# Attention scores built by adding key differences onto an older bank: one row-maximum product for two key tiles instead of eight

## The reference, cut to what matters

```python
src_trans = (einsum('bsf,of->bso', src, W_src) + b_src) * src_mask[:, :, None]   # keys and values
tgt_trans = (einsum('btf,of->bto', layernorm(x), W_tgt) + b_tgt) * tgt_mask[:, :, None]
scores = einsum('bthd,bshd->bhts', q, k) / sqrt(64)
scores = where(src_mask == 0, -inf, scores)
attn = softmax(scores, axis=-1)
tgt_update = einsum('bhts,bshd->bthd', attn, v)
x = x + tanh(g_xattn) * (concat([tgt, tgt_update]) @ W_out.T + b_out)
x = x + tanh(g_ffn) * bit_linear(silu(conv1d(bit_linear(layernorm(x), w1))), w2)
```

## Time and profile before

| what | value |
|---|---|
| median of 3 runs | 1748.87 us (1747.53 to 1750.27) |
| the profiled execution's own time | 1751.08 us |
| its span | 1749.3 us |
| PE busy | 1644.8 us, 94% |
| DVE, ACT, POOL busy | 1137.5, 836.4, 724.3 us |
| mean granted clock of PE | 0.981 |
| HBM read, written | 124.75 MB, 74.71 MB |

### The profile page before, as it was taken

How to read it: one execution, slowest core, us unless ns; L and a number is a source line. 1 busy time by engine, 2 the same in 40 slices (tenths; PEclk the granted TensorE clock), 3 DMA queues, 4 the chain that set the end, 5 groups by cost and what they waited for, 6 DMA issues and landing times. The chain is left out here.

```text
span 1749.3 us, 23957 instructions
## 1 busy us (share of the span) xinstructions
PE 1644.8 (94%) x8754; PEld 1009.1 (58%) x8754; DVE 1137.5 (65%) x2183; ACT 836.4 (48%) x901; POOL 724.3 (41%) x314
## 2 busy tenths in 40 slices
PE   6999999999998999999999999999999878797978
PEld 5788788888885544455444544454446444454544
DVE  7787634444436667656876677657734977969493
ACT  3233312222210344434564355524565988879776
POOL 1231000000000488856786577756871624426160
PEclk9999999999999999999999999999999989899989
DMA  7787555444434411113132133202143211020302
GB/s 258 267 278 247 195 182 184 164 165 163 161 144 151 152 62 62 65 69 110 62 110 97 57 114 110 86 2 109 54 156 119 71 55 37 23 75 1 97 0 79
DMA packets 109480, 200.88 MB, mean 115 GB/s; under 512 B 9280, under 2 KB 34880, under 8 KB 109376
## 3 DMA queue, kind: packets, MB, share of 16 engines
q1 hardware_dynamic: 109376, 199.50, 32.9%
HBM read 124.75 MB, written 74.71 MB: 114 GB/s over the span
## 5 line engine op out<-in xcount | busy, mean ns | idle before, releaser
L791 POOL TENSOR_TENSOR acc<-acc,pr 128x1024 f32<-128x1024 f32 x188 | 448.7, 2387 | 130.5 <-ACT pr L821 113.9
L821 ACT ACTIVATE pr<-ps,mcol 128x1024 f32<-128x1024 f32 x256 | 284.5, 1115 | 362.9 <-PE ps L1591 357.7
L1110 DVE CUSTOM_DVE_ANT_0 junk<-ps,mbias 128x512 bf16<-128x512 f32 x512 | 333.1, 689 | 129.8 <-PE ps L1566 125.4
L1603 PE MATMUL ps<-pr,vv 128*64 128x512 f32 x1024 | 273.8, 616 | 0.0
L798 POOL TENSOR_TENSOR h_first<-h_first,last_tap 128x1023 f32<-128x1023 f32 x43 | 105.3, 2451 | 177.0 <-DVE h_first L1443 146.4
L772 POOL MEMSET nmt<- 128x128 f32 x1 | 0.2, 205 | 343.4 <-DVE chl L1344 343.4
L1566 PE MATMUL ps<-kh,qh 64*128 64x512 f32 x512 | 123.1, 452 | 11.0 <-DVE nmv L1110 9.8
L791 POOL TENSOR_TENSOR acc<-pr 128x1024 f32<-128x1024 f32 x32 | 76.9, 2402 | 122.5 <-ACT pr L821 122.5
L1566 PEld LDWEIGHTS ps<-kh,qh 64*128 64x128 f32 x512 | 50.9, 184 | 128.7 <-issue 99.4
L1848 PE MATMUL ps<-w2q,hq 128*128 128x512 bf16 x512 | 123.0, 395 | 1.5 <-ACT hq L1002 0.7
L1691 PE MATMUL ps<-xiT,w1q 128*128 128x512 bf16 x512 | 121.2, 380 | 2.7 <-DVE x2t L1472 2.7
(11 more groups left out here) (175 smaller groups left out, 3147.1 us busy)
## 6 DMA issues: line engine op xcount, KB each, us to landing
craw<-in_ctxT SPq DMA_DIRECT2D x8, 2048.0 KB, 8.9
xa<-in_x SPq DMA_DIRECT2D x32, 256.0 KB, 3.9
wraw<-in_w1T SPq DMA_DIRECT2D x16, 512.0 KB, 5.9
wraw<-in_w2T SPq DMA_DIRECT2D x16, 512.0 KB, 6.6
q_split<-kqh SPq DMA_DIRECT2D x32, 256.0 KB, 2.1
q_split<-kql SPq DMA_DIRECT2D x32, 256.0 KB, 2.4
base<-lna SPq DMA_DIRECT2D x32, 256.0 KB, 3.7
k_split<-kqh SPq DMA_DIRECT2D x32, 256.0 KB, 2.0
```

The costliest lines, as they stand in the source:

```text
L791: nc.gpsimd.tensor_tensor(acc[:, blk % 2, :], first, pr[:, (8 * blk + j) % NP, :], ALU.add).then_inc(pool_acc, 1)
L821: act.activation(pr[:, u % NP, :], ps[:, 2 * (u % 2):2 * (u % 2) + 2, :].rearrange("p a t -> p (a t)"), ACT.Exp, bias=mcol[:, (u // 64) * ...
L1110: dve.tensor_tensor_reduce(out=(junk1 if n < LEAD and n % 2 else junk)[:, e, :], in0=ps[:, first_bank(n) + e, :], in1=mbias[:, b % 2, kk * ...
L1603: last = pe.matmul(ps[64 * e:64 * e + 64, 6 + blk % 2, :], vv[g % 2][:, j, 64 * e:64 * e + 64], pr[:, u % NP, e * CH:(e + 1) * CH], start= ...
```

## The change: what it does

For a block of queries, the scores of key tile `j` are now `S_j = S_{j-2} + q·(k_j - k_{j-2})` for `j` from 2 to 7. The banks of unit `u` are those of unit `u-2`, and they still hold `S_{j-2}` with the row maximum in it, so the first matmul doesn't start the bank anew (`start=j < 2 and w == 0`) and the product `aug1·maug` is sent for tiles 0 and 1 alone. Three products are left for the other six.

The differences are made in stage B. For each `m`, once the full key has been rounded (`kqh`, which `pe_tops` still needs), DVE makes the difference to the key tile two before, in two operations of 256 columns (in an odd chunk the first one needs the last 256 columns of the chunk before, kept in `carry`), ACT rounds it (`kdh`) and copies the new `carry`, and DVE makes the remainder. SP stores three parts, and `load_lo` loads three.

For room in SBUF `acc` moves to where `w2q` is loaded later, `vv0` and `kd_hi1` take its place, and `kdh` and `carry` lie over `qh1` and `kh1`. So `load_qk(1)` now stands behind the last chunk's key stores, `load_vv(0)` behind the whole of stage B, and the load of `w2q` also waits for the last `sums`.

```diff
-    kd = nc.dram_tensor("k_split", (B * PAIRS, 2, P, S), F32).ap()
+    kd = nc.dram_tensor("k_split", (B * PAIRS, 3, P, S), F32).ap()
...
             def load_lo(g):
...
+                sp.dma_start(kd_hi[g % 2][:].bitcast(F32), kd[g, 2]).then_inc(sp_lo[g % 2], 16)
...
-                    for w, t in ((0, kqh), (1, kql)):
+                    for w, t in ((0, kqh), (1, kql), (2, kdh)):
...
+                if last and half:
+                    for sl in range(2):
+                        sp.wait_ge(sp_k_out[sl], 48 + 96 * NCH)
+                    sp.wait_ge(act_b, c * B_ACT_N + B_ACT[f"cy{PAIRS - 1}"])
+                    load_qk(1)
...
             load_mrow(0)
-            load_qk(1)
             sp.dma_start(mcol[:], mask_cols).then_inc(sp_mcol, 16)
             load_lo(0)
-            for sl in range(2):
-                sp.wait_ge(sp_v_out[sl], 16 + 32 * (NCH - 1))
-            load_vv(0)
             b_chunk(B - 1, 1, True)
...
             sp.wait_ge(pe_bv, NCH * CT + 8)
+            load_vv(0)
             sp.wait_ge(dve_b, NCH * B_DVE_N)
...
+            sp.wait_ge(pe_z, 2 * NG)
             sp.dma_start(w2q[:], w2q_d.rearrange("(k p) o -> p k o", p=P)).then_inc(sp_w2, 16)
...
                     act.activation(kqh[:, m % 2, :], kq[:, m % 2, :], ACT.Copy).then_inc(act_b, 1)
+                    act.wait_ge(dve_b, c * B_DVE_N + B_DVE[f"db{m}"])
+                    act.activation(kdh[:, m % 2, :], kql[:, m % 2, :].bitcast(F32), ACT.Copy).then_inc(act_b, 1)
+                    act.activation(carry[:, m, :], kq[:, m % 2, 2 * P:CH], ACT.Copy).then_inc(act_b, 1)
...
+            def key_steps(dn, an, m, half):
+                diff, keys = kql[:, m % 2, :].bitcast(F32), kq[:, m % 2, :]
...
+                if half:
+                    dve.tensor_tensor(diff[:, 0:2 * P], keys[:, 0:2 * P], carry[:, m, :], ALU.subtract).then_inc(dve_b, 1)
+                else:
+                    dve.tensor_copy(diff[:, 0:2 * P], keys[:, 0:2 * P]).then_inc(dve_b, 1)
+                dve.tensor_tensor(diff[:, 2 * P:CH], keys[:, 2 * P:CH], keys[:, 0:2 * P], ALU.subtract).then_inc(dve_b, 1)
...
-                terms = ((kh[g % 3][:, keys], qh[g % 3][:, tokens]), (kl[g % 2][:, keys], qh[g % 3][:, tokens]),
-                         (kh[g % 3][:, keys], ql[g % 2][:, tokens]), (aug1[:], maug[g % 2][:, tokens]))
+                terms = ((kd_hi[g % 2][:, keys], qh[g % 3][:, tokens]), (kl[g % 2][:, keys], qh[g % 3][:, tokens]),
+                         (kd_hi[g % 2][:, keys], ql[g % 2][:, tokens]), (aug1[:], maug[g % 2][:, tokens]))
+                if j >= 2:
+                    terms = terms[0:3]
...
-                                         start=w == 0, stop=w == 3)
+                                         start=j < 2 and w == 0, stop=w == len(terms) - 1, skip_group_check=True)
```

More of the change, by code:

```diff
@@ L133, in flamingo_gated_block @@
         maskc = sb("maskc", [P, NCH * CT], F32)
+        kdh = sb("kdh", [P, 2, CH], F32R)
+        carry = sb("carry", [P, PAIRS, 2 * P], F32)
         assert used["at"] <= CRAW
@@ L160, in flamingo_gated_block @@
         used["at"] = TOP_AB
-        vv, ql, kl, maug = [], [], [], []
+        kd_hi, vv, ql, kl, maug = [], [], [], [], []
         for i in range(2):
-            vv.append(sb(f"vv{i}", [P, NT, P], F32))
+            if i == 0:
+                kd_hi.append(sb("kd_hi0", [P, S], F32R))
+            else:
+                vv.append(sb("vv1", [P, NT, P], F32))
             ql.append(sb(f"ql{i}", [P, S], F32R))
@@ L168, in flamingo_gated_block @@
                 assert used["at"] == TOP_AB + SLOT
-                acc = sb("acc", [P, 2, 2 * CH], F32)
+                vv.append(sb("vv0", [P, NT, P], F32))
+                kd_hi.append(sb("kd_hi1", [P, S], F32R))
         mbias = sb("mbias", [P, 2, S], F32)
@@ L197, in flamingo_gated_block @@
         xic = sb("xic", [P, NT, D], BF16)
+        acc = sb("acc", [P, 2, 2 * CH], F32)
+        assert used["at"] <= TOP_W
         used["at"] = XN + 4 * NT * D + 8 * S
@@ L344, in flamingo_gated_block @@
         n = 0
-        for name in ([f"{w}{m}" for m in range(PAIRS) for w in ("k", "kl")]
+        for name in ([f"{w}{m}" for m in range(PAIRS) for w in ("k", "da", "db", "kl")]
                      + [w + str(j // 2 if w[0] == "w" else j) for j in range(CT)
@@ L350, in flamingo_gated_block @@
         B_DVE_N = n
-        B_ACT = {name: i + 1 for i, name in enumerate([f"kh{m}" for m in range(PAIRS)]
+        B_ACT = {name: i + 1 for i, name in enumerate([f"{w}{m}" for m in range(PAIRS) for w in ("kh", "dh", "cy")]
                                                       + [f"vh{j}" for j in range(CT)])}
@@ L962, in _ @@
             for sl in range(2):
-                act.sem_inc(sp_k_out[sl], 32)
+                act.sem_inc(sp_k_out[sl], 48)
             act.wait_ge(pe_ab, NCH * CT + CT)
@@ L1344, in split_lo, with key_low @@
                     dve.tensor_tensor(chl[:, slot, k, :], craw[:, k, :], chh[:, slot, k, :].bitcast(F32), ALU.subtract).then_inc(dve_cl, 1)
+            def key_steps(dn, an, m, half):
+                diff, keys = kql[:, m % 2, :].bitcast(F32), kq[:, m % 2, :]
+                dve.wait_ge(act_b, an + B_ACT[f"kh{m}"])
+                dve.wait_ge(dve_b, dn + B_DVE[f"k{m}"])
+                if half:
+                    dve.tensor_tensor(diff[:, 0:2 * P], keys[:, 0:2 * P], carry[:, m, :], ALU.subtract).then_inc(dve_b, 1)
+                else:
+                    dve.tensor_copy(diff[:, 0:2 * P], keys[:, 0:2 * P]).then_inc(dve_b, 1)
+                dve.tensor_tensor(diff[:, 2 * P:CH], keys[:, 2 * P:CH], keys[:, 0:2 * P], ALU.subtract).then_inc(dve_b, 1)
+            def key_low(dn, an, m):
+                dve.wait_ge(act_b, an + B_ACT[f"dh{m}"])
+                dve.wait_ge(dve_b, dn + B_DVE[f"db{m}"])
+                dve.tensor_tensor(kql[:, m % 2, :], kql[:, m % 2, :].bitcast(F32), kdh[:, m % 2, :].bitcast(F32), ALU.subtract).then_inc(dve_b, 1)
             def b_chunk(b, half, last):
@@ L1355, in b_chunk @@
                         dve.wait_ge(dve_b, dn + B_DVE[f"kl{m - 2}"])
+                        dve.wait_ge(act_b, an + B_ACT[f"cy{m - 2}"])
                     dve.scalar_tensor_tensor(out=kq[:, m % 2, :], in0=ps[:, m, :], scalar=bk[:, m:m + 1], in1=maskb[:],
                                              op0=ALU.add, op1=ALU.mult).then_inc(dve_b, 1)
-                    dve.wait_ge(act_b, an + B_ACT[f"kh{m}"])
-                    dve.wait_ge(dve_b, dn + B_DVE[f"k{m}"])
-                    dve.tensor_tensor(kql[:, m % 2, :], kq[:, m % 2, :], kqh[:, m % 2, :].bitcast(F32), ALU.subtract).then_inc(dve_b, 1)
+                    key_steps(dn, an, m, half)
+                    key_low(dn, an, m)
                 for j in range(CT):
```

16 lines of the change are left out of this document (8 added, 8 removed).

## The result

The changed kernel takes 1721.43 us (median of 4 runs, 1718.66 to 1723.04) against 1749.47 us for the kernel before (4 runs, 1747.53 to 1750.27): a ratio of 0.984, 95% interval 0.9822 to 0.9857, or 28.0 us less. The profiled execution took 1719.99 us (span 1718.2), 31.1 us less than that of before. The forecast was 1710, with a range of 1701 to 1722. The direction and the main mechanism were right; the gain was 11 us smaller than the 39 forecast. In two later groups of runs, each with its own kernel before, the gain was 33.1 and 31.0 us, so the shortfall is 6 to 11 us.

What follows compares the result with a forecast made beforehand. The prediction took stage C to be bound by what PE sends. Its terms, -44.2 + 4 + 1.5 + 1 - 2.5 + 1.5 = -38.7 us, gave 1710 us: forecast 1703 to 1719, wider range 1701 to 1722.

Steps and rivals of the forecast that it cites:

- What PE sends (-44.2): Stage C: six units in eight lose one pair of matmuls, 192 x 0.23 = 44.2 us less.
- Small operations at the layer norms (+4): Macros 53 and 85: POOL's closer adds make both sequences meet a long small DVE operation, not just one: +4 us.
- In macros 43 to 47 (+1.5: Macros around 44, where `lower` was held: 0.5 us less given back in each of three sequences, +1.5 us.
- The tail (+1): End of stage C, no tops left: POOL's 17.7 us a block exceed PE's need, lag grows; +1 us, bounds 0 and 4.
- The last chunk (-2.5): Start of stage B's last chunk: earlier `mcol` load shortens PE's 4.61 us idle; -2.5 us, bounds 0 and -4.5.
- `vv` (+1.5): Start of stage C: later `load_vv(0)` makes the first product wait; +1.5 us, bounds +0.5 and +5.
- Stage B (0): Added DVE and ACT steps fit in DVE's 3.30 us wait for PE ahead of each key group: cost 0.
- POOL (0): Stage C: adds at 2.52 us pitch need 17.7 of 18.4 us, queue empties once a block: cost 0.
- Rivals one: Stage C: `lower` meets a POOL add in every block, 2.2 us each: 1778 us; 5 in 100.
- rival two: Stage C: POOL becomes the bound; at a pitch of 2.75 us the time is 1735 us; 8 in 100.
- Rival three: Small holds (both layer norm sequences, `vv` wait, end of stage C), each with half clock, add up: 1720 to 1728; 10 in 100.

Runs made afterwards that it cites:

- two of them: Kernel before, without key differences, with fewer small DVE operations in the diagonal layer norms and the last chunk's weights load issued later, behind the masks: 1743.36 us, ratio 0.9959.
- the small operations changed: Changed kernel with the four small DVE operations ending each layer norm of stage C cut to two, one factor made by ACT: 1714.16 us, ratio 0.9798.
- all three together: Changed kernel with three repairs: tops one pair later, fewer small layer norm operations, last chunk's weights behind the masks and `vv` before the last value store: 1702.03 us.

## Why the prediction was off by 11 us

**What PE sends (-44.2).** Right as a mechanism: 0.23 us came out wherever PE was not made to wait, also for the pairs that add onto an old bank, and with the three repairs on one side and two of them on the other 41.4 of the 44.2 could be had.

**Tops behind `sums` and `project` (not in the sum).** This is the step that failed. The prediction said that "what is taken out of its list is taken out of the time, as long as the next engine is far enough away", looked at POOL, at `lower` and at DVE's busy share, and took the DVE operations ahead of the plain tops as free. It did not look at the place in PE's list where the removed pair stood between a DVE reading of bank 4 or 5 and the tops that write that bank again. There the pair had been cover: without it PE is held by the end of DVE's operation for under 0.1 us to 0.2 us, and pays 0.11 more since the tops' weight load, which had run under the removed pair, now delays the pair behind them. The table gives 2.7 us in the 14 macros behind `sums`, 4.3 in the 24 with `project` and most of the 2.0 in macros 43 to 47: about 8 us. Sending those tops a pair later gave 6.6 of them back. The same loss in the kernel that only leaves the products out, and PEld's rows, which come and go with the cover, leave no other cause.

**Small operations at the layer norms (+4).** Both were hit, as said, but not for the reason given, POOL's adds closer together: with the pairs taken out and nothing else one of the two was hit, as before, and with no pair taken out but the new stage B both were. So the size was right and the hit on the second sequence was luck; what sets the phase is not shown. Macros 54 and 86 fell short of the pairs taken out by 3.7 us, all six by 4.9, a part of which is late tops. In macros 43 to 47 (+1.5, for `lower` held longer) about 1 us is left once the late tops are taken off; `lower` took less time there than before (2.2 us, not 2.88), which doesn't fit the reason given, and the cause of this 1 us stays open.

**The tail (+1)** cost nothing: the last ten macros gave their pairs in full.

**The last chunk (-2.5).** The idle time became 2.49, as said ("about 2.4"), the new one of 1.19 was spoken of only as extra steps "with tops waiting". The sum from the start of stage B to the first exponential is -3.5, as this execution also had no half clock there (1.00 against 0.94). The profiled executions of the kernel with stage B alone and of that with the small operations changed did have it (0.94 in the first), and in the changed kernel's two other profiled executions the same sum is -0.6, with half clock, and -3.2, without.

**`vv` (+1.5).** 0.80 us of recorded wait, 1.1 us missing in the first four macros.

**Stage B (0)** was right: PE is busy 293.67 of 294 us with the extra work in the kernel with stage B alone, and DVE still waits 1.97 us for PE in a group of the changed kernel. **POOL (0)** was right: a pitch of 2.52 us, queue empty once a block. Rivals one (`lower`, 0.69 to 0.94 us in plain blocks) and two are out; the sum of rival two comes to 1737 with its own terms, not 1735. Rival three, 1720 to 1728, has the right total, but its holds were the ones already in the sum; those that made the difference were in none of the cases. So 1721.43 lies outside the 1703 to 1719 of the forecast and inside the wider range, by 0.6 us, which takes in part of rival three: that the range held is luck in part.

The sum with the measured terms: -44.2 + 8 (late tops) + 4.5 (macros 53 to 55 and 85 to 87, late tops off) + 1 (43 to 47) + 1.1 (start of C) - 3.5 = -33.1, against 31.1 in the profiled pair. The plain macros with two pairs less gave 0.43 instead of 0.46 each, 1 us in all. Most of that is a third, smaller case of the same lost cover, which the later tops don't mend: at 11 places the tops wait for `mt`, DVE's read of the turned row maxima (PEld's row `DVE mt L1146` has 2.5 us in 11 waits, and the pair behind the tops starts 0.30 instead of 0.23 us later, 0.8 us in all). The last 1 us stays open. Outside this sum stage A was 1.8 us longer in this pair of executions and what follows the last exponential 1.8 us shorter; in stage A the stretches at half clock add up to 3.4 us more, behind the scores to 3 us less, which accounts for most of both.

What stays open is the clock: why a stretch of half clock follows one idle time and not another. Between two executions of one kernel in one group it is worth up to 8 us, and it blurs every comparison of medians here of less than 2 to 3 us.

## What to carry to other kernels

Before an instruction on the bounding engine is counted as gain, look at what its neighbours in the list wait for: where it stands between another engine's last reading of a bank and the next write to it, it is cover, and its time comes back as a wait that the matmul rows of the waits view don't show. Look at the rows of the weight load too, compare the starts in the timeline and not the listed idle times, and move the writer behind independent work. Small holds that each cost little are best judged together: in these runs the kernels with one repair still had the half clock behind the idle times that were left, and their medians showed less than the parts were worth. And when a foreseen hit comes, try the kernel without its supposed cause.

## What the runs showed that was not expected

A wait of PE under 0.1 us cost 0.18: the tops pair behind it is listed with 0.50 instead of 0.39 us and the next pair starts 0.34 instead of 0.23 us later, since the weight load starts only with the tops. The first score pair behind a product has the same 0.50 and 0.34 (1031.50 and 1031.84 in the changed kernel).

Half clock follows an idle time only sometimes, and the length of the idle time doesn't tell it: in one execution of the changed kernel it came at 1056.40 after 2.26 us and did not come at 872.96 after 2.28 us. In the profiled execution of all three together it came after 0.94 us (granted clock 0.56 from 815 to 817); the product behind it took 1.85 us, where 1.08 is usual:

```profile
812.01 1.08 PE L1640 MATMUL ps<-pr,vv 128*64 128x512 f32 x4
814.04 1.11 PE L1599 MATMUL ps<-kh,qh 64*128 64x512 f32 x2 [0.94 <-DVE nmv L1131]
815.08 1.85 PE L1640 MATMUL ps<-pr,vv 128*64 128x512 f32 x4
```

The second execution of that kernel had no such stretch between the last chunk and the end of the scores.
